# A hybrid layer (Mamba-2 block and 4-bit MLP) on one core: the first loads and the written-out order of all engines changed

## What is computed

```python
def mamba2(u):                       # u: 4 x 1024 x 256
    z, xBC, dt = split(u @ in_proj)                    # 512, 512 + 2*128, 8 columns
    x, B, C = split(silu(causal_conv1d(xBC, taps=4)))
    dt = softplus(dt + dt_bias); A = -exp(A_log)       # 8 heads of 64
    S = 0                            # state: 128 x (8 heads x 64)
    y[t] = C[t] @ S + x[t] * D, with S = S * exp(A*dt[t]) + B[t] (x) (dt[t]*x[t])   # in chunks
    y = y * silu(z)
    return (y * rsqrt(mean(y*y) + eps) * norm_w) @ out_proj

def mlp(x):                          # weights: 4-bit codes and a scale per 32
    g, up = x @ dequant(gate).T, x @ dequant(up).T     # 256 -> 2048
    return (gelu_tanh(g) * up) @ dequant(down).T       # 2048 -> 256

x = u + layernorm(mamba2(layernorm(u)))
out = x + layernorm(mlp(layernorm(x)))
```

## Time and profile before

| | |
|---|---|
| median of 3 runs | 960.33 us (960.23 to 961.1) |
| the profiled execution | 961.48 us |
| its span, first to last instruction | 959.8 us |
| PE, DVE, ACT, POOL busy | 889.1, 752.7, 618.5, 355.3 us |
| mean granted TensorE clock | 0.984 of full speed |
| a whole iteration of `ORDER` | 109.3 us |

### The profile page before, as it was taken

How to read it: one execution, slowest core, us unless ns; L and a number is a source line. 1 busy time by engine, 2 the same in 40 slices (tenths; PEclk the granted TensorE clock), 3 DMA queues, 4 the chain that set the end, 5 groups by cost and what they waited for, 6 DMA issues and landing times.

```text
span 959.8 us, 17690 instructions
## 1 busy us (share of the span) xinstructions
PE 889.1 (93%) x6400; PEld 776.2 (81%) x6400; DVE 752.7 (78%) x2031; ACT 618.5 (64%) x1034; POOL 355.3 (37%) x342
## 2 busy tenths in 40 slices
PE   4388889999999999999999999999999999999987
PEld 3368687889897888888898898988888898888886
DVE  5988999787888697887888788787978888786232
ACT  5857887857759385765858395774858485673222
POOL 2031526253343525253342616243442525244323
PEclk9589999999999999999999999999999999999999
DMA  7501010201002010200102010110102010010000
GB/s 224 183 1 56 1 57 2 67 1 44 14 12 67 1 56 1 78 1 14 45 13 66 2 56 1 45 34 13 45 13 67 1 56 2 23 45 2 1 23 12
DMA packets 19206, 34.59 MB, mean 36 GB/s; under 512 B 2480, under 2 KB 11440, under 8 KB 19120
## 3 DMA queue, kind: packets, MB, share of 16 engines
q1 hardware_dynamic: 18256, 33.44, 11.1%
q10 hardware_dynamic: 864, 0.03, 0.1%
HBM read 29.14 MB, written 4.33 MB: 35 GB/s over the span
## 4 chain that ended last, share of the span: by engine, by line
PE 62%; DVE 16%; ACT 11%; issue 5%; POOL 3%; DMA 1%; SPq 0%; POOLq 0%; DVEq 0%; ACTq 0%
PE fb L1083 27%; PE db L1083 14%; PE mb L1083 10%; DVE xc L891 3%; PE mb L1199 3%; PE mb L1190 3%; ACT L711 2%; POOL hl L589 2%; ACT hid L711 2%; PE mb L1180 1%; ACT xc L671 1%; PE mb L1205 1%; ACT xc L664 1%; DVE st L1008 1%; ACT L671 1%
## 5 line engine op out<-in xcount | busy, mean ns | idle before, releaser
L589 POOL TENSOR_TENSOR hl<-hid,hl 128x512 fp32r<-128x512 f32 (+1 forms) x144 | 183.8, 1281 | 344.5 <-ACT hl L718 344.3
L1083 PE MATMUL fb<-x1t,wg 128*128 128x512 f32 (+1 forms) x864 | 213.5, 382 | 5.6 <-DVE x1t L994 2.9
L1083 PE MATMUL db<-wd,hl 128*128 128x256 f32 x1536 | 217.6, 291 | 0.7 <-POOL hl L589 0.7
L1083 PE MATMUL fb<-x1t,wu 128*128 128x512 f32 (+1 forms) x864 | 202.7, 370 | 13.4 <-ACT hid L711 13.3
L1083 PEld LDWEIGHTS db<-wd,hl 128*128 128x128 f32 x1536 | 195.7, 191 | 15.2 <-issue 10.5
L1083 PEld LDWEIGHTS fb<-x1t,wu 128*128 128x128 f32 x864 | 149.8, 189 | 48.9 <-ACT hid L711 22.7
L1083 PEld LDWEIGHTS fb<-x1t,wg 128*128 128x128 f32 x864 | 146.1, 189 | 37.4 <-issue 10.1
L711 ACT ACTIVATE hid<-fb 128x512 f32<-128x512 f32 (+1 forms) x144 | 78.4, 550 | 129.8 <-PE fb L1083 115.5
L891 DVE SCALAR_TENSOR_TENSOR xc<-raw,cw,xc 128x256 f32<-128x256 f32 x288 | 135.7, 539 | 5.3 <-ACT xc L664 3.2
L1000 DVE TENSOR_TENSOR hid<-fb,hid 128x512 f32<-128x512 f32 (+1 forms) x144 | 90.0, 626 | 58.9 <-PE fb L1083 34.2
L559 POOL TENSOR_TENSOR rs<-ve,neg_half 128x1 f32<-128x1 f32 (+2 forms) x89 | 62.0, 697 | 168.0 <-DVE ve L793 62.5
(11 more groups left out here) (143 smaller groups left out, 1319.8 us busy)
## 6 DMA issues: line engine op xcount, KB each, us to landing
lmat<-rows SPq DMA_DIRECT2D x32, 512.0 KB, 4.4
xin<-in_u SPq DMA_DIRECT2D x16, 256.0 KB, 2.7
out<-xb SPq DMA_DIRECT2D x16, 256.0 KB, 2.2
wg_raw<-in_packed SPq DMA_DIRECT2D x4, 256.0 KB, 13.2
wg_raw<-in_scales SPq DMA_DIRECT2D x4, 256.0 KB
wu_raw<-in_packed SPq DMA_DIRECT2D x4, 256.0 KB, 12.3
wu_raw<-in_scales SPq DMA_DIRECT2D x4, 256.0 KB
wd_raw<-in_packed SPq DMA_DIRECT2D x4, 256.0 KB, 13.2
```

The costliest lines, as they stand in the source:

```text
L589: pool.tensor_tensor(hl[:, hs, n % 2, 1, :], hid[:, hs, n % 2, :], hl[:, hs, n % 2, 0, :].bitcast(F32), ALU.subtract).then_inc(s["lo"], 1)
L1083: last = pe.matmul(ps, lhs(a, k), rhs(b, k), start=start and n == 0, stop=stop and n == len(todo) - 1, skip_group_check=check)
```

## The change

Two things. The loads: the first piece's words and scales are issued ahead of the z columns of in_proj, the first x rows of block 1 behind the second piece, and out_proj's weights behind the fifth piece (they were ahead of the first). And the orders: `FIRST`, `ORDER` and `LAST` are written anew for PE, ACT, DVE and POOL (`LAST` for PE and ACT only). No step is added or taken away, and no instruction inside a step is changed; the Mamba steps of `ORDER` take the same `mb` banks. In `FIRST`, `dq:0` and `scale:0` of DVE now stand ahead of its `wi_split`, and no `warm` step stands ahead of `xt:1`. The function `warm` also moves to another place in the file.

The diff, with `ORDER`, `FIRST` for PE and the loads whole, and the start of `FIRST` for ACT and DVE:

```diff
 
 ORDER = {
     "pe": """
-        gu:0< gu:1< cs:0 gu:2< ct:0 dn:0< gu:3< xtr:0 gu:4< dn:1< gb:0 dn:2< gu:5< yo:0 yd:0 dn:3< st:0 gu:6<
-        yt:0 xtr:1 dn:4< out:0 yo:1 dn:5< yd:1 st:1 gu:7< xt:1 yt:1 gu:8< ip:3 out:1 z:3 z:4 dn:6< gu:9< dn:7<
-        ip:4 cs:1 ip:5 gu:10< ct:1 z:5 gu:11< gu:12< dn:8< gb:1 yo:2 dn:9< xtr:2 xt:0> gu:13< dn:10< yd:2 dn:11<
-        st:2 yt:2 xtr:3 gu:14< out:2 yo:3 dn:12< yd:3 st:3 gu:15< yt:3 dn:13< x1t:0 out:3 z:0> z:1> dn:14<
-        dn:15< ip:0> x1t:1 ip:1> z:2> ip:2>""",
+        cs:0 gu:0< gu:1< gu:2< dn:0< gu:3< ct:0 xtr:0 gb:0 dn:1< yo:0 gu:4< dn:2< yd:0 gu:5< st:0 yt:0 xtr:1
+        dn:3< out:0 yo:1 yd:1 gu:6< st:1 gu:7< xt:1 yt:1 dn:4< ip:3 dn:5< out:1 z:3 z:4 gu:8< dn:6< gu:9< ip:4
+        cs:1 ip:5 gu:10< z:5 ct:1 dn:7< gu:11< gb:1 yo:2 dn:8< xtr:2 gu:12< dn:9< xt:0> yd:2 dn:10< st:2 gu:13<
+        yt:2 xtr:3 dn:11< out:2 yo:3 yd:3 gu:14< dn:12< st:3 yt:3 gu:15< out:3 z:0> dn:13< z:1> x1t:0 dn:14<
+        dn:15< x1t:1 ip:0> ip:1> z:2> ip:2>""",
     "act": """
-        gelu:0< gelu:1< split:0< silu:0 gelu:2< silu:1 gate:2 split:1< split:2< gelu:3< silu:2 gelu:4< exps:0
-        decay_matrix:0 decay_matrix:1 decay_matrix:2 split:3< split:4< gb_copy:0 decay_matrix:3 gelu:5< split:5<
-        yt_split:0 square:0 gelu:6< gelu:7< yt_split:1 split:6< xn_split:1 split:7< taps:3 square:1 gelu:8<
-        gate:3 gate:4 dt_bias:1 gelu:9< split:8< taps:4 taps:5 gelu:10< split:9< gate:5 gelu:11< silu:3 silu:4
-        silu:5 decay_matrix:4 decay_matrix:5 split:10< gb_copy:1 exps:1 decay_matrix:6 gelu:12< split:11<
-        xn_split:0> decay_matrix:7 square:2 gelu:13< yt_split:2 split:12< gelu:14< split:13< gelu:15< split:14<
-        square:3 yt_split:3 split:15< dt_bias:0> gate:0> x1_split:0 gate:1> x1_split:1 taps:0> taps:1> taps:2>""",
+        gelu:0< gelu:1< split:0< gate:2 silu:0 gelu:2< silu:1 split:1< silu:2 gelu:3< split:2< decay_matrix:0
+        exps:0 decay_matrix:1 gelu:4< split:3< gb_copy:0 gelu:5< decay_matrix:2 yt_split:0 decay_matrix:3
+        split:4< square:0 gelu:6< split:5< square:1 xn_split:1 yt_split:1 split:6< taps:3 gelu:7< gelu:8<
+        dt_bias:1 split:7< gate:3 gate:4 gelu:9< taps:4 split:8< taps:5 gelu:10< gate:5 silu:3 split:9< silu:4
+        silu:5 decay_matrix:4 decay_matrix:5 gelu:11< decay_matrix:6 split:10< gb_copy:1 exps:1 decay_matrix:7
+        xn_split:0> gelu:12< split:11< split:12< gelu:13< yt_split:2 square:2 split:13< square:3 gelu:14<
+        split:14< yt_split:3 gelu:15< split:15< dt_bias:0> gate:0> gate:1> x1_split:0 x1_split:1 taps:0> taps:1>
+        taps:2>""",
     "dve": """
-        inter:0< decays:0 inter:1< conv:1 inter:2< conv:2 sums:0 xdt:0 decay_sums:0 inter:3< decay_sums:1
-        inter:4< gb_copy:0 decay_sums:2 decay_sums:3 decayed_products:0 stats1:1 yoff:0 ydiag:0 inter:5<
-        decayed_products:1 state:0 yt_split:0 xdt:1 stats2:0 xn:1 yoff:1 ln2:0 ydiag:1 inter:6< inter:7< state:1
-        yt_split:1 xn_split:1 stats2:1 dt_bias:1 ln2:1 conv:3 softplus:1 inter:8< stats1:0> decays:1 inter:9<
-        conv:4 inter:10< xn:0> conv:5 sums:1 inter:11< decay_sums:4 decay_sums:5 decay_sums:6 gb_copy:1
-        decayed_products:2 xdt:2 yoff:2 inter:12< x1n:0 xn_split:0> decay_sums:7 ydiag:2 decayed_products:3
-        x1n:1 state:2 yt_split:2 xdt:3 inter:13< stats2:2 yoff:3 inter:14< ln2:2 ydiag:3 state:3 yt_split:3
-        inter:15< stats2:3 x1n:2 dt_bias:0> ln2:3 softplus:0> x1n:3 fin:0< x1_split:0 x1_split:1 conv:0> ln4:0<""",
+        decays:0 inter:0< conv:1 inter:1< conv:2 inter:2< stats1:1 sums:0 decay_sums:0 decay_sums:1 xdt:0
+        decay_sums:2 gb_copy:0 decayed_products:0 yoff:0 inter:3< inter:4< ydiag:0 decay_sums:3 state:0 inter:5<
+        yt_split:0 decayed_products:1 xdt:1 stats2:0 yoff:1 ln2:0 state:1 xn:1 ydiag:1 xn_split:1 inter:6<
+        yt_split:1 conv:3 inter:7< stats2:1 dt_bias:1 ln2:1 softplus:1 stats1:0> inter:8< inter:9< decays:1
+        conv:4 conv:5 inter:10< sums:1 decay_sums:4 decay_sums:5 gb_copy:1 decay_sums:6 decayed_products:2
+        decay_sums:7 xdt:2 xn:0> inter:11< yoff:2 xn_split:0> inter:12< state:2 ydiag:2 inter:13< yt_split:2
+        decayed_products:3 xdt:3 yoff:3 stats2:2 ydiag:3 x1n:0 ln2:2 inter:14< x1n:1 state:3 yt_split:3
+        inter:15< stats2:3 ln2:3 dt_bias:0> x1n:2 x1n:3 softplus:0> fin:0< x1_split:0 x1_split:1 conv:0> ln4:0<""",
     "pool": """
-        split:0< split:1< split:2< xdt:0 split:3< yoff:0 split:4< stats1:1 split:5< stats2:0 xdt:1 yoff:1
-        split:6< split:7< ln2:0 stats2:1 stats1:0> split:8< split:9< split:10< xdt:2 yoff:2 split:11< ln2:1
-        split:12< xdt:3 stats2:2 yoff:3 split:13< ln2:2 split:14< split:15< stats2:3 ln2:3 fin:0<""",
+        split:0< split:1< split:2< xdt:0 yoff:0 split:3< split:4< xdt:1 stats2:0 stats1:1 yoff:1 split:5<
+        split:6< ln2:0 stats2:1 split:7< split:8< stats1:0> split:9< xdt:2 split:10< yoff:2 ln2:1 split:11<
+        xdt:3 yoff:3 split:12< stats2:2 ln2:2 split:13< split:14< stats2:3 split:15< ln2:3 fin:0<""",
 }
...
 FIRST = {
     "pe": """
-        warm:0 xt:1 ip:3 warm:1 z:3 z:4 warm:2 ip:4 ip:5 cs:1 ct:1 z:5 warm:3 xtr:2 gb:1 warm:4 yo:2 warm:5
-        xt:0> st:2 warm:6 yd:2 warm:7 xtr:3 yt:2 warm:8 yo:3 out:2 yd:3 warm:9 yt:3 warm:10 st:3 out:3 z:0>
-        warm:11 z:1> warm:12 warm:13 ip:0> ip:1> warm:14 warm:15 cs:0> x1t:1 warm:16 ip:2> warm:17 z:2> warm:18
-        ct:0> warm:19 gu:0 gu:1 warm:20 xtr:0> gb:0> gu:2 yo:0> warm:21 warm:22 gu:3 warm:23 dn:0 st:0> yd:0>
-        gu:4 dn:1 yt:0> xtr:1> dn:2 gu:5 out:0> yo:1> gu:6 yd:1> dn:3 xt:1> st:1> dn:4 yt:1> dn:5 ip:3> out:1>
-        gu:7 gu:8 z:3> z:4> ip:4> gu:9 dn:6 dn:7 cs:1> ip:5> z:5> gu:10 dn:8 gu:11 dn:9 xtr:2> ct:1> yo:2> gb:1>
-        gu:12 xt:0>> dn:10 st:2> yd:2> gu:13 xtr:3> yt:2> dn:11 gu:14 yo:3> dn:12 out:2> yd:3> gu:15 x1t:0>
-        yt:3> st:3> dn:13 out:3> z:0>> z:1>> dn:14 dn:15 ip:0>> ip:1>> x1t:1> ip:2>> z:2>>""",
+        xt:1 ip:3 z:3 z:4 warm:0 ip:4 z:5 warm:1 xtr:2 cs:1 ip:5 warm:2 warm:3 ct:1 gb:1 yo:2 warm:4 xt:0> st:2
+        yd:2 warm:5 xtr:3 warm:6 yt:2 warm:7 warm:8 warm:9 yo:3 out:2 yd:3 warm:10 warm:11 warm:12 yt:3 st:3
+        out:3 warm:13 warm:14 z:0> z:1> warm:15 warm:16 ip:0> ip:1> ip:2> x1t:1 warm:17 cs:0> warm:18 z:2>
+        warm:19 gu:0 ct:0> warm:20 gu:1 warm:21 warm:22 gu:2 xtr:0> gb:0> warm:23 dn:0 gu:3 dn:1 st:0> yo:0>
+        yd:0> gu:4 dn:2 yt:0> xtr:1> gu:5 yo:1> out:0> yd:1> xt:1> gu:6 dn:3 yt:1> st:1> dn:4 ip:3> out:1> z:3>
+        gu:7 gu:8 z:4> dn:5 ip:4> gu:9 dn:6 dn:7 ip:5> cs:1> gu:10 ct:1> gu:11 z:5> dn:8 xtr:2> dn:9 yo:2> gb:1>
+        gu:12 xt:0>> st:2> yd:2> dn:10 yt:2> xtr:3> gu:13 yo:3> out:2> yd:3> dn:11 gu:14 yt:3> gu:15 st:3> dn:12
+        out:3> z:0>> z:1>> dn:13 x1t:0> dn:14 ip:0>> dn:15 x1t:1> ip:1>> z:2>> ip:2>>""",
     "act": """
-        wi_split:0 wi_z:0 xn_split:1 rates:0 dq:0 taps:3 dq:1 silu:3 dl:0 dq:2 taps:4 dq:3 dq:4 dt_bias:1 gate:3
-        dl:1 gate:4 dl:2 dq:5 taps:5 dq:6 dq:7 dl:3 gate:5 silu:4 dq:8 silu:5 wo_split:0 dq:9 exps:1
-        decay_sums:4 decay_sums:5 decay_matrix:4 gb_copy:1 decay_matrix:5 decay_sums:6 decay_matrix:6
...
+        wi_split:0 xn_split:1 dq:0 wi_z:0 dq:1 rates:0 taps:3 dq:2 taps:4 gate:3 gate:4 dq:3 dq:4 dq:5 dl:0
+        silu:3 dt_bias:1 dq:6 silu:4 dl:1 gate:5 wo_split:0 dq:7 dq:8 dl:2 dl:3 taps:5 dl:4 dq:9 silu:5 exps:1
+        decay_sums:4 gb_copy:1 decay_sums:5 decay_matrix:4 decay_matrix:5 decay_sums:6 xn_split:0>
...
     "dve": """
-        stats1:1 xn:1 xn_split:1 wi_split:0 dq:0 rates:0 scale:0 conv:3 dt_bias:1 dq:1 stats1:0> dq:2 conv:4
-        wo_split:0 dl:0 scale:1 scale:2 dq:3 dq:4 softplus:1 dq:5 decays:1 scale:3 dq:6 scale:4 conv:5 scale:5
-        xn:0> dl:1 scale:6 dq:7 sums:1 wo_lo:0 dl:2 gb_copy:1 xdt:2 decayed_products:2 yoff:2 xn_split:0>
-        state:2 ydiag:2 decayed_products:3 dl:3 yt_split:2 xdt:3 yoff:3 stats2:2 ydiag:3 ln2:2 yt_split:3
-        state:3 dq:8 scale:7 stats2:3 dt_bias:0> x1n:2 ln2:3 softplus:0> x1n:3 conv:0> dl:4 decays:0> x1_split:1
...
+        stats1:1 xn:1 dq:0 scale:0 wi_split:0 xn_split:1 stats1:0> dq:1 scale:1 rates:0 dt_bias:1 conv:3 dq:2
+        conv:4 scale:2 dq:3 dq:4 softplus:1 wo_split:0 scale:3 scale:4 dq:5 dq:6 decays:1 dq:7 xn:0> dl:1 conv:5
+        xdt:2 wo_lo:0 dq:8 sums:1 dl:0 gb_copy:1 scale:5 yoff:2 decayed_products:2 state:2 xn_split:0> ydiag:2
+        scale:6 decayed_products:3 yt_split:2 xdt:3 yoff:3 stats2:2 ydiag:3 ln2:2 yt_split:3 dl:6 state:3 x1n:2
+        stats2:3 dl:4 dt_bias:0> ln2:3 softplus:0> x1n:3 conv:0> conv:1> x1_split:1 decays:0> dl:5 scale:7
...
 LAST = {
     "pe": """
-        gu:0< gu:1< gu:2< gu:3< dn:0< dn:1< gu:4< dn:2< gu:5< dn:3< gu:6< dn:4< gu:7< gu:8< dn:5< dn:6< gu:9<
-        dn:7< gu:10< gu:11< dn:8< dn:9< gu:12< gu:13< dn:10< dn:11< gu:14< dn:12< gu:15< dn:13< dn:14< dn:15<""",
+        gu:0< gu:1< gu:2< dn:0< gu:3< dn:1< gu:4< dn:2< dn:3< gu:5< gu:6< dn:4< gu:7< dn:5< gu:8< gu:9< dn:6<
```

(28 more changed lines are left out.)

58 lines of the change are left out of this document (29 added, 29 removed).

## The result

The changed kernel takes 950.87 us (median of four runs, 947.98 to 951.72), the kernel before, run beside it, 960.67 (960.23 to 961.1): ratio 0.9895, 95% interval 0.9882 to 0.9908. It is 9.8 us faster; 954.0 was forecast. The profiled execution took 950.83, its span is 949.1 where it was 959.8. One of the later executions of the kernel before took 991.91 us, at a mean granted clock of 0.866 where the others had 0.98 or more, and is left out of all medians and ratios.

A forecast was written before the change was run, and what follows sets the result against it. DVE's weight unpacking bounds the first 148 us, then PE, nearly full, idling 2.02 us per whole iteration. Iterations -7.0, half iteration -0.5, opening +1.0, end 0 make -6.5 us: 954 us forecast, range 946.5 to 962.

The forecast's parts named there:

- A: Whole kernel: the three gelu waits go, smaller ones stay, opening about even; 948.5 to 958.4 us, chance 0.54.
- the three gelu waits: PE's waits for ACT's gelu ahead of up halves of gu:1, gu:4, gu:13: 0.39, 0.66, 0.78 us, all to go.
- the opening: Stretch before the repeated iterations, new FIRST and loads: 1.0 us later, between -1.5 and +3.
- the end: New LAST: one of two PE waits at the tail goes, worth 0, at most 0.3 us either way.
- the second part: Second gelu wait, 0.66 us ahead of gu:4's up half: goes, as ct:0, xtr:0, gb:0, dn:1, yo:0 stand ahead.
- 0.85 us left in each iteration: PE wait remaining of 2.02 us per whole iteration; 1.17 less, six times, gives 7.0 us gain.
- The wait of 0.5 us ahead of `out:0`: New PE wait in each iteration: decayed_products:0 on DVE meets POOL's state decay, delaying split:3 and yt_split:0; 0.5 us.
- The 0.3 at `dn:10`, `dn:12` and `st:3`: Small PE waits late in each iteration, behind POOL's splits and ln2:2: 0.3 us together.
- The half iteration: Seventh iteration, without a second Mamba half: 0.5 us off its 1.3 us of PE idle.
- B: Whole kernel: all iteration waits go and the opening gains; 945.5 to 948.5 us, chance 0.14.
- C: Iteration waits only change places, 1.7 to 2.2 us each, opening +0 to 1; 958.4 to 962.2 us, chance 0.15.
- D: POOL's queue in each iteration's first third delays out:0 by 1.5 us; slower, 966.6 us, chance 0.17.

The follow-up runs named there:

- e6: Changed kernel with gu:4 back directly behind xtr:0 in PE's ORDER list, ahead of gb:0, dn:1 and yo:0: 956.70 us, ratio to before 0.9966.
- e2: Kernel before with only the new FIRST and the new loads: 964.94 us, ratio to before 1.0045.
- e7: Changed kernel with gu:13 moved ahead of yd:2, dn:10 and st:2 in PE's ORDER list: 982.18 us, ratio to before 1.0227.
- e1: Kernel before with only the new ORDER, all engines' lists: 948.46 us, ratio to before 0.9884.
- e4: Kernel before with the new ORDER and the new LAST: 949.30 us, ratio to before 0.9889.
- e10: Kernel before with the new ORDER lists of PE, ACT and VectorE but POOL's old one: 1053.65 us, ratio to before 1.0966.
- e9: Kernel before with the new ORDER list of PE alone: 1169.21 us, ratio to before 1.2165.
- e8: Changed kernel with VectorE's second wi_split and xn_split:1 ahead of scale:0 in FIRST: 947.12 us, ratio to before 0.9861.
- e5: Changed kernel with VectorE's dl:2 moved ahead of stats1:1, sums:0 and dq:9 in FIRST: 949.10 us, ratio to before 0.9882.
- e11: Changed kernel with both moves of e5 and e8 in VectorE's FIRST list: 947.82 us, ratio to before 0.9867.

## Why the prediction was right, and where its sizes were off

The forecast was A, 948.5 to 958.4: the three gelu waits go, the opening costs a little. It holds. The measured -9.8 is 3.3 us more than the -6.5 of the sum. The terms miss by more than that, and in part against each other: in the profiled execution the iterations gave 4.5 us more than the 7.0 forecast and the half one 1.2 more, while the opening cost 1.1 more and the end 0.5.

**The three gelu waits.** All gone, by the mechanism given, and nearly at the times given. `taps:2` was laid out to end at t = 1.5 and gelu:0 at 3.4; they end at 502.45 (1.9 from 500.57) and 504.35 (3.8). gelu:3 was to be done at 15.4 to 16.2:

```profile
514.30 1.28 ACT L715 ACT_TABLE_LOAD   x1 [0.91 <-POOL hl L593]
515.59 0.60 ACT L715 ACTIVATE hid<-fb 128x512 f32<-128x512 f32 x1
```

It is done at 516.2, t = 15.6, where it was 16.2 before, and the group that waits for it now comes at t = 17.5. e6 takes the second part back and pays 0.9 us an iteration.

**The term that was mis-sized: 0.85 us left in each iteration.** (Its parts, 0.5 and 0.3, make 0.8; the last 0.05 has no row.) Measured: 0.21 idle by the windows, and no wait listed. The wait of 0.5 us ahead of `out:0` was argued from a meeting of VectorE and POOL, and the meeting took place:

```profile
519.86 2.02 POOL L578 TENSOR_TENSOR state<-state,ex 128x512 f32<-128x512 f32 x1
```

```profile
519.34 1.65 DVE L914 TENSOR_TENSOR lmat<-lmat,gb 128x1024 f32<-128x1024 f32 x1 [0.25 <-ACT lmat L657]
...
527.55 0.69 DVE L953 TENSOR_TENSOR yt<-mb,yt 128x512 fp32r<-128x512 f32 x1
```

The decay took 2.02 us in place of 1.04: 1.0, as I had taken it. `yt_split:0` of VectorE ends at 528.24, t = 27.67; I had 27.6. What was wrong is the other side. PE reaches `out:0` at t = 27.7, and I had laid it out to be there at 27.15. The chain of the supply was right to 0.1 us, and PE's own way there was 0.5 to 0.6 us too short, the size of the wait. From the up half of `gu:4`, at 17.5 where I had 17.4, most of that was lost; on which of the steps, the working does not show. It is close: `out:0` starts 0.05 us behind the end of `yt_split:0`.

The 0.3 at `dn:10`, `dn:12` and `st:3` also came to nothing, but by the supply. POOL's `split:10` ends at 574.08 and `split:12` at 587.69, t = 73.5 and 87.1, where I had 73.9 and 87.4, and `dn:10` and `dn:12` start without a wait at 574.14 and 587.89. Here PE was 0.4 and 0.1 earlier than I had it, too. Edges that come out by 0.05 to 0.2 us were not foreseen by a laying out that is right to some tenths; that all of them fell on the good side is in part luck.

Six times 0.64 (0.85 less 0.21) is 3.8 us of the 4.5. The rest is near what PE's busy time fell by, 107.12 in place of 107.28 an iteration.

The Trainium skill (SBUF — State Buffer, "Who interferes with whom") has a VectorE instruction with two SBUF inputs and a GpSimd instruction that reads SBUF exclude each other on a shared port, for a whole instruction. The 16-column product, 2.34 us beside POOL's and 0.17 without it, agrees with that. The decay, 0.98 us longer beside a product of 1.65, does not tell the rule from the 1.0 that I took.

**The half iteration.** -1.72 us, and I had -0.5. One wait of 0.28 is left in it ahead of the 2.73 of the end, so again less was left than I had laid out; its edges are not broken down.

**The opening: +1.0 forecast, +2.08 at `gu:0` in the profiled execution.** The order of events is as laid out: first piece's words at 8.54 (8.4), no `wi_split` before them. `ip:3` came at 16.87, not 15.7. I had priced `wi_split` at 2.96 + 0.16 us from the earlier trace rows, and that row itself holds a meeting: POOL's z part ran from 9.51 to 11.91 then, and without it the step takes 1.75 (above). After the change that meeting is gone, and another one, of 2.17 us, is at the 16 columns. One row taken as a plain duration hid both. `ydiag:2` ended at 61.16 in place of 58.5, so the opening was 3.4 us behind there; 1.3 of it came back. The wait of 2.82 us ahead of `dn:0` is one that I did not name. VectorE's list has `sums:0`, which waited 1.69 us for a DMA, and `dq:9`, which nobody needed yet, ahead of `dl:2`. A low clock follows it (below). The bounds, -1.5 to +3, held in the profiled execution. In the three others with this opening it is +0.1 (e2), +3.2 (e6) and +4.0 (e7), the last two above the bounds and e7's above the 180 that was to refute the forecast: the term had no allowance for how much the opening varies by itself. e2's other three times lie 2 to 3 us above its profiled one; an opening like that of e6 or e7 would do it, which is not shown.

**The end.** `LAST` was put at 0, with one of the two last waits taken away. Ahead of `dn:15` there is one wait of 0.65, and e1, with the old `LAST`, has 0.16 and 0.24. The 0.46 us by which the stretch is longer in the profiled execution is the clock's: 0.90 over it, where it was 0.96. e4, with the new `LAST` at 0.96, has 43.19 us there, and before had 43.18.

**The rivals.** B (everything goes and the opening gains) describes the iterations; the opening and the clock at the end kept the time out of it. C and D needed waits at `out:0`, `dn:10` and `dn:12` that came to nothing. e10 shows that D's place, POOL's queue ahead of `yoff`, is a real danger, and at another order of the same few steps it costs many times what I gave it.

## What to carry to other kernels

When orders are laid out against each other, lay out both sides of each edge with the same care: half a microsecond on the side of the bound engine's own steps is as much as half a microsecond of supply, and at an edge it decides. Before a landmark of one profile is called the gain of an edit, look at how far it moves between executions in which nothing ahead of it was changed (here 4 us). Read a duration with what the neighbour was doing: a row may hold a meeting of VectorE and POOL, and a move can take it away or make a worse one on an instruction of 0.17 us. An engine that is busy for 37% of the time can still set the end by its order (105 us here). A list laid out anew needs the lists that it was laid out with (e9, e10); single steps can be moved alone, for better (e8) or worse (e7).

## What the runs showed of the hardware

The granted clock falls behind a wait of TensorE in some executions, and not in others. Windows of the changed kernel (the clock is the third number from the end); the wait of 2.82 us ends at 97.89:

```profile
90.00:95.00 5.00, 4.74 (x40) 4.41 (x38) 3.58 (x14) 4.94 (x8) 1.43 (x2) 1.00 0.70 210
95.00:100.00 5.00, 2.18 (x11) 2.11 (x11) 4.59 (x10) 4.63 (x10) 1.08 (x1) 0.73 0.00 0
100.00:105.00 5.00, 4.25 (x29) 2.97 (x30) 5.00 (x7) 4.97 (x13) 1.97 (x2) 0.93 0.00 0
```

`dn:0` takes 1.65 us in this place, in e5 0.96: part of it ran at 1.2 GHz, the lower of the two levels, and not at 2.4. In e6, with the same opening, it takes 0.98 behind a longer wait, of 2.97 us, and the granted clock from 95 to 100 us is 1.00. At the start of `LAST` the groups behind the wait of 2.73 us take 1.47 to 1.48 us in the changed kernel and 0.88 in e5. The wait is the same in both, so the length of the wait alone doesn't decide it.

The times of one kernel lie up to 4 us apart (e11: 945.85 with a mean granted clock of 0.987, 949.60 with 0.981). Such a fall of the clock and the DMA ahead of `sums:0` are two things seen to differ between profiles; as there is one profile of each kernel, which of them is behind its slower times is not shown. A difference below 4 us needs more runs than the four or five of each kernel here, or a range as narrow as e8's (2.3 us).

The landing of the z columns moved by 2.2 us between executions of the same load order (ACT's copy began at 11.54 in e6, 12.33 in the changed kernel, 13.65 in e8, 13.76 in e5). Where two engines' steps meet can hang on it. The order of e8 and e11 takes `wi_split` out of its way, so that `ip:3` came at 13.24 and 13.30 with the columns at 13.65 and 11.72. The meeting itself is not gone: in e11 POOL's part began at 12.86, and VectorE's `scale:0`, which `ip:3` does not wait for, took 3.34 us in place of 1.28.
